# Missing edges of a second block group, subtracted by GpSimd instead of by a mask product on TensorE

## The reference, cut to what matters

```
h = relu(layernorm(x));  x = x + relu(h @ W_S.T + b_S + segment_sum((h[src] @ W_N.T + b_N) * exp(-w), dst))
h = relu(layernorm(x))
q, k, v = h @ Wq + bq, h @ Wk + bk, h @ Wv + bv
logits = sum(q[dst] * k[src], -1) / sqrt(128);  m = segment_max(logits, dst)
ex = exp(logits - m[dst]);  alpha = ex / segment_sum(ex, dst)[dst]
x = x + elu(segment_sum(alpha[:, None] * v[src], dst) + h @ W_skip + b_skip)
```

## Time and profile before

| | |
|---|---|
| median of 3 runs | 868.57 us |
| profiled execution | 869.26 us |
| its span, first to last instruction | 867.5 us |
| mean granted TensorE clock | 0.974 |
| busy, TensorE / VectorE / ScalarE / GpSimd | 87% / 87% / 59% / 30% |
| stage 4, from 529.4 us to the end | 338 us |
| one tile step in the middle of stage 4 | 12.6 us |

### The profile page before, as it was taken

The page is one execution under the profiler, slowest core; times in us unless marked ns, Lnnn a source line. Parts: engine busy times, 40 slices in busy tenths (PEclk is TensorE's granted clock), DMA queues, the critical chain, the costliest instruction groups (busy, mean ns, idle before and its releaser), DMA issues.

```text
span 867.5 us, 22993 instructions
## 1 busy us (share of the span) xinstructions
PE 756.2 (87%) x8799; PEld 654.9 (75%) x8846; DVE 754.6 (87%) x908; ACT 510.7 (59%) x1034; POOL 256.3 (30%) x199
## 2 busy tenths in 40 slices
PE   0064799999999999999999787799999999999996
PEld 0052677777777777777777466699999999999996
DVE  6647999999999999999996556799999999999982
ACT  5954667667676776767766243344554555455444
POOL 5640000000000000000000230366667667666766
PEclk9997899999999999999999799699999999999999
DMA  9540113123132131221312441204244334423400
GB/s 232 142 135 2 78 78 147 81 83 144 76 132 94 76 151 76 123 104 76 151 76 113 163 180 61 92 1 155 86 154 157 124 113 156 157 94 142 157 7 11
DMA packets 17516, 94.96 MB, mean 109 GB/s; under 512 B 2594, under 2 KB 8844, under 8 KB 10956
## 3 DMA queue, kind: packets, MB, share of 16 engines
q1 hardware_dynamic: 14428, 89.18, 27.0%
q0 software_dynamic: 3056, 5.35, 2.7%
HBM read 50.31 MB, written 44.21 MB: 109 GB/s over the span
## 4 chain that ended last, share of the span: by engine, by line
PE 59%; DVE 11%; issue 11%; POOL 4%; ACT 2%; DMA 2%; DVEq 1%; SPq 0%; POOLq 0%; ACTq 0%
PE bank L1041 14%; PE bank L1182 13%; PE bank L1192 12%; DVE oh_key L873 6%; PE bank L1031 5%; PE bank L1103 5%; PE bank L1101 5%; POOL sm L458 3%; DVE kT L777 3%; DMA gl_sb<-gt 2%; PE bank L1145 1%; PE bank L1179 1%; PE bank L1150 1%; DVE mx L960 1%; DVE oh_lo L870 1%
## 5 line engine op out<-in xcount | busy, mean ns | idle before, releaser
L458 POOL TENSOR_TENSOR sm<-sm,mbc 128x896 f32<-128x896 f32 (+1 forms) x100 | 186.3, 1896 | 74.1 <-ACT mbc L647 74.1
L1101 PE MATMUL bank<-oh_key,oh_lo 128*128 128x100 bf16 x1600 | 172.2, 209 | 13.5 <-DVE oh_key L873 11.8
L1041 PE MATMUL bank<-wsb,hvb 128*128 128x512 f32 (+1 forms) x350 | 166.2, 580 | 13.7 <-DVE kT L777 12.4
L1182 PE MATMUL bank<-qT,kT 128*128 (+1 forms) x1250 | 167.9, 279 | 7.3 <-issue 3.9
L1103 PE MATMUL bank<-oh_key,oh_lo 128*128 128x50 bf16 x3200 | 172.5, 187 | 0.0
L1101 PEld LDWEIGHTS bank<-oh_key,oh_lo 128*128 128x128 bf16 x1600 | 156.3, 98 | 19.6 <-DVE oh_key L873 12.4
L1182 PEld LDWEIGHTS bank<-qT,kT 128*128 128x128 f32 x1250 | 163.7, 196 | 5.0 <-DVEq L173 1.2
L1103 PEld LDWEIGHTS bank<-oh_key,oh_lo 128*128 128x128 bf16 x3200 | 165.5, 98 | 1.1
L554 ACT COPY wsb<-bank 128x512 f32<-128x512 f32 (+1 forms) x175 | 88.1, 553 | 106.3 <-PE bank L1031 106.3
L1192 PE MATMUL bank<-vals,sm 128*128 128x129 f32 x1250 | 147.5, 274 | 0.2 <-ACT sm L651 0.2
L960 DVE TENSOR_REDUCE mx<-sm 128x128 f32<-128x3200 f32 x25 | 146.2, 5847 | 0.9
(11 more groups left out here) (120 smaller groups left out, 707.1 us busy)
## 6 DMA issues: line engine op xcount, KB each, us to landing
gt<-gst SPq DMA_DIRECT2D x25, 1600.0 KB, 5.6
gl_sb<-gt SPq DMA_DIRECT2D x25, 1600.0 KB, 6.8
records<-rec SPq DMA_DIRECT2D x1, 1612.0 KB
out<-res SPq DMA_DIRECT2D x24, 64.0 KB, 1.6
dst_i<-in_dst SPq DMA_DIRECT2D x1, 403.0 KB, 5.7
dstn_i<-in_dst_next SPq DMA_DIRECT2D x1, 403.0 KB, 6.6
src_i<-in_src SPq DMA_DIRECT2D x1, 403.0 KB, 7.2
w_in<-in_edge_weight SPq DMA_DIRECT2D x1, 403.0 KB, 7.8
```

The costliest lines, as they stand in the source:

```text
L458: pool.tensor_tensor(part, part, mbc[:, v % 2:v % 2 + 1, :].to_broadcast([P, n, P]), ALU.subtract).then_inc(sub_done, 1)
L1041: T.matmul(ps(6 + at)[:, 0:n], hvb[:, w, :], wsb[:, at, 0:n], start=True, stop=True).then_inc(l0_mm, 1)
L1101: T.matmul(cells, lo, oh_key[:, u, m, 0:2 * KEYS, i], start=True, stop=False, skip_group_check=True)
L1182: ins = T.matmul(score_bank(g)[:, j * P:(j + 1) * P], kT[:, (a + j) * P:(a + j + 1) * P], qT[:, bass.ds(t * P, P)], start=g < LIFT, stop=T ...
```

## The change

Group 1 is taken off TensorE's mask product. `LIFT` becomes 2, which in the code means: TensorE issues no L1179 for groups 0 and 1, and `absent` covers only groups 2 and 3. ScalarE's `mark_absent` issues two instructions: one writes `steep` = relu(-2^60 * gl) of group 1 in fp32 (a new buffer with two slots), the other writes `absent` of groups 2 and 3. GpSimd gets a new function, `lift_second`, which waits for `steep` and subtracts it from group 1 of `gl_sb` in place, one 128x768 instruction. VectorE's mask of group 1 waits for that. VectorE's own lift of group 0 stays.

```diff
-LIFT = 1
+LIFT = 2
...
-        past_gl = sb(s2, "past_gl", [P, (P + KEYS) * (QN - TWO)], BF16)
+        past_gl = sb(s2, "past_gl", [P, (P + KEYS) * (QN + TWO)], BF16)
...
+        steep = sb(s4, "steep", [P, 2, SG[1][1] * P])
...
+            def lift_second(t, v):
+                a, n = SG[1]
+                part = gl_sb[:, v, a * P:(a + n) * P]
+                pool.wait_ge(steep_ready, t + 1)
+                pool.tensor_tensor(part, part, steep[:, v % 2, :], ALU.subtract).then_inc(lifted_p, 1)
+
+            lift_second(0, 0)
+
             def pool_step(t, v, uses):
 
+                if live(t + 1):
+                    lift_second(t + 1, (v + 1) % RING)
                 if live(t - 1):
                     subtract_max(t - 1, (v - 1) % RING)
...
                     act.wait_ge(s_ready, (t - 1) * NSG)
+                if not isinstance(t, int) or t >= 2:
+                    act.wait_ge(lifted_p, t - 1)
+                a, n = SG[1]
+                nc.scalar.activation(steep[:, v % 2, :], gl_sb[:, v, a * P:(a + n) * P], ACT.Relu, scale=-STEEP).then_inc(steep_ready, 1)
                 nc.scalar.activation(absent[:, v % 2, LIFTED:], gl_sb[:, v, LIFTED:], ACT.Relu, scale=-STEEP).then_inc(absent_ready, 1)
...
                 if g < LIFT:
-                    dve.wait_ge(lifted, t * LIFT + g + 1)
+                    dve.wait_ge((lifted, lifted_p)[g], t + 1)
...
-            for g in range(LIFT):
-                lift(0, 0, 0, g)
+            lift(0, 0, 0, 0)
```

More of the change, by code:

```diff
@@ L278, in build_gnn @@
         gl = [sem(f"gl{k}") for k in range(RING)]
-        absent_ready, lifted = sem("absent_ready"), sem("lifted")
+        absent_ready, lifted, lifted_p, steep_ready = (sem(n) for n in ("absent_ready", "lifted", "lifted_p", "steep_ready"))
         s_ready, masked, mx_ready, mt_ready, m_ready, dg_ready, mb_ready, mbc_ready = (
```

## The result

The changed kernel takes 875.82 us (median of 5 runs, 874.6 to 877.95) against 868.49 us (5 runs, 866.88 to 869.34). The ratio is 1.0083, with a 95% interval of 1.0068 to 1.0099: slower by 0.8%, about 7.3 us. Predicted were 876.3 us, between 869 and 882, slower with a chance of 0.83.

What follows compares the result with a forecast made beforehand. TensorE was taken to bound the steady steps at 12.63 us, GpSimd and ScalarE's loop afterwards at 12.90. Terms 0.3 + 1.7 + 6.5 - 0.8 = +7.7 us gave 877.0 profiled, 876.3 as median; range 869 to 882.

Steps and rivals of the forecast that it cites:

- The loop of GpSimd and ScalarE: Steady steps of stage 4: with the new instruction and ScalarE's split this loop takes 12.90 us and sets the step.
- the lower bound from L449: GpSimd's new instruction: at least 1.51 us, scaled from a 128x640 instruction of 1.256 us with one input constant along the row.
- VectorE's loop of 12.43: Steady steps of stage 4: VectorE's chain through masks, reduction, lift and TensorE's group 3 scores takes 12.43 us.
- TensorE's saving: Steady steps: dropping group 1's mask product frees 0.33 us a tile on TensorE, of which only 0.19 can be had.
- VectorE tied to GpSimd: Steady steps: VectorE's lift, ready 0.47 us earlier, is held until GpSimd's subtraction ends, taking 1.6 to 1.8 us, not 1.28.
- rival 4: Steady steps: VectorE slips past a whole subtraction piece and delays exponentials by 1.08 us a step, about 897 us; chance 0.05.
- Late loads: First steps of stage 4: ScalarE's waits for gl_sb make two steps exceed 12.90 by 0.41 and 0.81 us, +1.2.
- The start: Start of stage 4: GpSimd's new instructions for tiles 0 and 1 meet VectorE's first two lifts, +1.7 us, between 0 and 2.7.
- rival 1: Stage 4's start and first subtractions: GpSimd wins every meeting with VectorE's lift, up to +4.6 us, 880.9 us; chance 0.17.
- the middle: Third to 23rd subtraction: 20 steps of 12.90 us plus 1.2 make 259.2 us for 252.7, +6.5 us.
- the last two steps: 23rd to 25th subtraction, without new instructions ahead of the last two subtractions: 21.8 us for 22.6, -0.8 us.
- I expect no fall for such gaps: TensorE's granted clock stays at the 2.4 GHz level although TensorE stalls about 0.6 us more in each step.

Runs made afterwards that it cites:

- e4: Changed kernel with ScalarE's instruction that writes steep moved from ahead of the fourth exponential to behind the row work; 866.56 us, ratio 0.9994 to the kernel before.
- e5: Changed kernel, but GpSimd takes only four of group 1's six blocks and TensorE keeps the mask product for the other two; 866.78 us, ratio 1.0003 to before.
- e2: Changed kernel with TensorE's mask product for group 1 put back, GpSimd's instruction and ScalarE's split kept; 876.64 us, ratio 1.011 to before.
- e1: Changed kernel with group 1's missing edges not lowered at all: no mask product, steep or GpSimd instruction; 862.26 us, ratio 0.9934 to before.
- e7: e4 with the new GpSimd instruction for tiles 0 and 1 issued at the end of GpSimd's work in stage 3; 865.13 us, ratio 0.9972 to before.
- e8: e7 with group 3 taken off TensorE's mask product in place of group 1; 861.62 us, ratio 0.9939 to before.
- e3: Changed kernel with GpSimd's new instruction moved between the subtraction and the row work, for a tile one further on; 891.25 us, ratio 1.0269 to before.
- e9: e3 with the diagonal's instruction reading its identity from a copy in PSUM instead of SBUF; 866.43 us, ratio 0.9993 to before.

## Why the prediction was right, and where not

*The loop of GpSimd and ScalarE* was 12.90 in the forecast and is 12.83. Its terms were 10.06 to L465's start (10.06 and 9.98 in these two steps), 1.04 to the new instruction (1.04 in both steps) and 1.79 behind it (1.77). The new instruction takes 1.81 to 1.82 us for the 1.83 of the nearest row; the lower bound from L449, 1.51, was 0.3 too low. The estimate of 1.69 from the Trainium skill, page "GPSIMD Engine Reference", section "Elementwise — side-by-side cycle accounting", was 0.12 too low. e4, e5 and e2 show the rest of the mechanism: shorten either half of the loop and the loss goes, give TensorE its work back and the steps stay. The split cost ScalarE 0.10 us for the forecast 0.13.

*VectorE's loop of 12.43* as what comes next is shown by e1, e4 and e7, all at 12.43, and by e8, which changes what lies on that loop. TensorE's saving was mis-sized: the 1.67 us of one score group included a gap of 0.05 ahead of its first row, and the product is 0.27 (see e8), not 0.33. It did not matter here, as only 0.19 could be had.

*VectorE tied to GpSimd* is right: its lift takes 1.62 and 1.73 us in turn, as said. Its lead reached 1.5 us once, in the step after a late load, where the lift took 2.59 us; a subtraction piece is 1.83, so it never slipped past one (rival 4; its sum, 876.3 + 21.6, makes 898 and not 897).

*Late loads* were forecast as two longer steps with 1.2 us in sum. There was one of 13.86 instead of 12.8, and one more near the end, 13.27, which nothing had announced. ScalarE waited for `gl_sb` in both, 0.87 us in the first, and in the second:

```profile
831.59 0.85 ACT L634 ACTIVATE steep<-gl_sb 128x768 f32<-128x768 f32 x1 [0.36 <-DMA gl_sb<-gt]
```

The step behind that one is 11.39 us for the 12.0 of the forecast, so a part of the -1.4 in the table only makes up for it.

*The start* was the weakest step. The meeting of the two lifts is real, but of the forecast 1.7 us only 1.1 reached the first subtraction: the second lift ended 1.3 later, counted from the start of the stage (535.42 for 533.54, and 0.6 less). And for the two meetings behind the first subtractions the text had only two outcomes, none or 1.83 each by rival 1, GpSimd going first. What happened is a third: VectorE's lift is let in, and the diagonal's instruction behind it is held for 1.24. I had not counted that instruction among those that GpSimd can hold. The profile of before has the hint, outside the rows that I had used: the last diagonal, the only one beside a subtraction, took 0.52 us for 0.29.

```profile
849.35 0.52 DVE L938 TENSOR_SCALAR diag<-ident,mcol 128x128 f32<-128x128 f32 x1
```

Net it cost 1.2 us from the first to the third subtraction, where the forecast had none. That the total came so near is in part luck, as the misses cancel: the start, the middle and the last two steps came out 0.6, 1.1 and 0.6 us under the forecast, and these 1.2, the 0.3 ahead of stage 4 and the 1.0 at the end over it. The direction and the length of a steady step are not luck.

*The end.* "I expect no fall for such gaps" held in the steady steps: the granted clock is 1.00 from 650 to 800 us. It fell behind the last subtraction, and not because of the gaps that the change makes. The same two stretches in both profiles, before and then after (stretch, busy us of TensorE, its weight loads, VectorE, ScalarE and GpSimd, clock share, DMA share, GB/s):

```profile
847.00:850.00 3.00, 0.96 (x7) 0.58 (x6) 2.51 (x5) 1.15 (x3) 2.78 (x2) 1.00 0.00 0
850.00:854.00 4.00, 4.00 (x36) 4.00 (x37) 0.48 (x2) 1.72 (x6) 2.72 (x3) 1.00 0.08 20
```

```profile
854.00:857.00 3.00, 0.96 (x7) 0.58 (x6) 2.51 (x5) 1.13 (x3) 2.77 (x2) 1.00 0.00 0
857.00:861.00 4.00, 4.00 (x22) 4.00 (x23) 0.47 (x2) 1.71 (x6) 2.73 (x3) 0.59 0.07 19
```

Ahead of the last subtraction TensorE works 0.96 us of 3 in both. Then the clock stays at 1.00 before, and after it is near the lower of its levels, 1.2 GHz, for 4 us, in which there are only 22 records of matmuls for 36. That is the 1.0 us behind the last subtraction, which begins 15.3 us ahead of the end before and 16.4 after. The profiles of e1, which has no new instruction at all, and of e2, e4 and e7 show the same fall and 16.3 to 16.4 us; those of e3, e5, e8 and e9 show none and 15.3. So this 1.0 us belongs to single executions and not to the change. What decides it stays open. The mean clock of a run does not tell (0.975 in e7 with the fall, 0.971 in e5 without), so how many of the five runs of the changed kernel had it is not known.

## What to carry to other kernels

Idle time of an engine is free only where the next thing on it waits for something outside; follow the loop through all engines that it crosses, and compare loops, not busy shares. A saving on the engine that bounds is worth at most the distance to the second longest loop, and work moved off it should be taken from the place where the other loops pass too (of the product's 0.27 us, 0.19 a step in group 1 and 0.23 in group 3). When VectorE and GpSimd work at the same time, look at every VectorE instruction with inputs in SBUF, short ones too, and compare its time with and without GpSimd beside it: here the lift and the diagonal's instruction were held, and the masks and the long reduction hardly or not at all. And before an effect at an edge of the kernel is put down to a change, look for it in the profiles of the variants without the change.

## What the runs showed of the hardware

- A 128x128 `tensor_scalar` in fp32 from SBUF, with one scalar a partition, takes 0.29 us alone and 1.52 when GpSimd is inside a 1.8 us instruction with two SBUF inputs; read from PSUM it takes 0.35 beside the same instruction.
- VectorE's mask with one input in PSUM and one in SBUF is not held: 896 columns take 1.09 us with GpSimd idle (at 531.45 us in the profile before) and 1.09 beside the subtraction (at 722.19). The reduction over 3200 columns in SBUF takes 5.58 alone (at 537.33) and 5.87 beside the subtraction (at 716.42).
- A VectorE instruction that is held by one GpSimd instruction is let in ahead of the next, though that one is ready behind it at once: at 559 us in the changed kernel, and in the steps of e3 and e9 that are shown above.
- GpSimd's `tensor_tensor` in fp32 took 1.81 us for 768 columns of two full inputs and 1.27 for 512, 2.1 ns a column; with an input that is constant along the row it was 1.256 for 640.
- After the same 3 us with 0.96 us of TensorE work, the granted clock of the next 4 us was 1.00 in the profile before and 0.59 in the changed kernel's.
